# Perceiver block kernel: query transposes and two maxima products of the second cross attention placed ahead of the first scores

## The chip, the cores and the metric

One core of one Trainium2 chip runs the whole kernel as one program. The metric is the device time of one execution in microseconds; the time before is the median of three runs. TensorE is called PE, VectorE DVE, ScalarE ACT and GpSimd POOL; SP issues most DMAs.

## The reference, cut to what matters

The model has two layers, each with a cross attention, a self attention and a mixture of experts. The change lies in the second layer's cross attention, with 512 tokens (8 batches of 64), a context of 1601 rows a batch, 16 heads of width 16, and one key and value head that all query heads share:

```
q = x @ Wq
kv = context @ Wkv
k, v = jnp.split(kv, 2, axis=-1)
q = q.reshape(b, n, h, hd).transpose(0, 2, 1, 3) * scale
sim = jnp.einsum('bhnd,btd->bhnt', q, k)
att = jax.nn.softmax(sim, axis=-1)
y = jnp.einsum('bhnt,btd->bhnd', att, v)
return y.transpose(0, 2, 1, 3).reshape(b, n, d) @ Wo
```

## The kernel before, in words

Every engine has its own list of instructions, written out by hand in order; semaphores (`mq[...]` in this stage) tie them together. There is no planner: the order in the source is the order of each engine.

Queries are split in parts of bfloat16 (`Qs`, 96 columns a head), turned by PE with the heads' columns on partitions, and copied by ACT from PSUM into `QT`. Token tile t (0 to 3) has 16 heads, turned in two halves, `turn_queries(t, h8, at)`: 8 transposes of 128 by 96 into bank `at`; ACT's `queries_turned` copies them (L750). Tile 0 is turned first, since everything needs it. The other six turns are in `QUERY_TURNS`, one at the end of each of the units 0 to 5, all into bank 6; so each waits for the copy of the one before.

A group g (0 to 15, `NH`) is 8 heads of one batch. The softmax's maximum for each group is found by `maxima`: 13 chunks (`CH`) of products of queries and keys, 12 of four matmuls with 512 columns (L1670) and a short one of 16 with 65 columns (L1676), alternately in banks 4 and 5. DVE reduces each (L1096, the short one L1098), and chunk n waits until the reduce of chunk n - 2 is done. After the 13th reduce DVE takes the negative maximum (L1106); for group 0 DVE splits it in two bfloat16 parts (L1109, L1110), for the others POOL does (L516, L517). `rows(g)` turns the parts into two more rows by PE (L1690, bank 6), ACT copies them behind the queries (`row`, L767), so that `scores` gives the scores less their maximum.

A unit u is a seventh (`HS`) of a group: `scores(u)` has 8 matmuls of 512 columns (L1702) in banks 0, 1 or 2, 3, ACT takes the exponential (L789), `values(u)` multiplies by the values (L1716). Loop pass u issues scores(u + 1), one maxima chunk, values(u - 1), the other chunks, and then the turn. `chunks_by(u)` says how many chunks are issued by the end of pass u: 13 before the loop, then 16, 19, 22, 25, 28, 31, 33 and on. At s_ = 5 of each group `rows(g + 1)` goes ahead of the scores.

Before the loop PE projects the queries, turns tile 0, and alternates the projections of the tiles 1 to 3 with two chunks each; then it runs chunks 8 to 12, `keep_clock(7, 7)` (7 matmuls of 128x512 into bank 7 that nobody reads, L1282), `rows(0)`, `keep_clock(2, 7)` and `scores(0)`. POOL prepares the parts of the tiles 1 to 3 meanwhile (L503 to L511).

Of the kernel before, what the change touches and what calls it, by code (L numbers as in the profile page):

```python
# [16 lines left out]
TT = TOK // P  # L17
# [12 lines left out]
NH, HS = 2 * NB, 7  # L30
# [3 lines left out]
CH = 13  # L34
# [24 lines left out]
def build(nc, a, out, scratch_x, scratch_y, scratch_g):  # L59
    with ExitStack() as ctx:  # L60
# [136 lines left out]
        def bank(i, n=512):  # L197
            return ps[:, i, 0:n]
# [12 lines left out]

        def chunks_by(u):

            return min(CH * NH, CH + 3 * (u + 1), 20 + -(-CH * (u + 1) // HS))

        QUERY_TURNS = {(0, s_): (1 + s_ // 2, s_ % 2) for s_ in range(2 * TT - 2)}

        def key_tiles(s):
            return [k for k in (2 * s, 2 * s + 1) if k < KT_N]
# [2 lines left out]
        def sems(prefix, names):  # L222
            return {n: sem(f"{prefix}_{n}") for n in names.split()}
# [21 lines left out]
        at = sems("attn", "sc z ex pt_ps pt pv y v0")  # L245
# [28 lines left out]
        mq = sems("mq", "neg ln xt_ps xt q_ps qhi qf qs qdup qt_ps qt qt_b a_ps a_max nm row_ps row s_ps exp pv o o_ps y y_ps yt out_ps x")  # L274
# [280 lines left out]
        def _(act):  # L555
# [181 lines left out]
            def scaled_queries(t):  # L737
                act.wait_ge(mq["q_ps"], t + 1)
                q_ps = bank((7, 6, 7, 0)[t], D).rearrange("p (h d) -> p h d", h=H)
                if t == 0:  # L740
                    act.mul(Qs[:, 0:H, 0:HD], q_ps, SCALE).then_inc(mq["qhi"], 1)
                    act.wait_ge(mq["qhi"], 1)
                    act.activation(Qs[:, 0:H, HD:2 * HD], Qs[:, 0:H, 0:HD], ACT.Copy).then_inc(mq["qf"], 1)
                    return
                act.mul(qf[:, t * H:(t + 1) * H, :], q_ps, SCALE)
                act.mul(Qs[:, t * H:(t + 1) * H, 0:HD], q_ps, SCALE).then_inc(mq["qf"], 1)

            def queries_turned(t, h8, at):
                act.wait_ge(mq["qt_ps"], 2 * t + h8 + 1)
                act.activation(QT[0:KQ, 2 * t:2 * t + 2, 8 * h8:8 * h8 + 8, :].rearrange("p b h q -> p h b q"),  # L750
                               ps[0:KQ, at, :].bitcast(BF16).rearrange("p (h b q) -> p h b q", h=8, b=2), ACT.Copy).then_inc(mq["qt"], 1)
# [9 lines left out]
            for t in range(1, TT):  # L761
                scaled_queries(t)
            act.activation(exp_warm[:], xnT[:, 0, 0:1], ACT.Exp)

            def row(g):
                act.wait_ge(mq["row_ps"], g + 1)
                act.activation(QT[KQ:KQ2, g // 2, 8 * (g % 2):8 * (g % 2) + 8, :],  # L767
                               ps[KQ:KQ2, 6, :].rearrange("p (h q) -> p h q", h=8), ACT.Copy).then_inc(mq["row"], 1)

            def sums_out(g):  # L770
                act.wait_ge(mq["pv"], HS * (g + 1))
                if g >= 2:
                    act.wait_ge(mq["o_ps"], g - 1)
                act.activation(oT[g % 2], bank(7, P), ACT.Copy).then_inc(mq["o"], 1)
# [6 lines left out]
            for g in range(NH):  # L781
                for s_ in range(HS):
                    u = g * HS + s_
# [7 lines left out]
                    if s_ == 0 and g >= 1:  # L791
                        sums_out(g - 1)
                    if (g, s_ - 1) in QUERY_TURNS:
                        queries_turned(*QUERY_TURNS[g, s_ - 1], 6)
                    if s_ == 4 and g >= 2 and g % 2 == 0:
# [49 lines left out]
        def _(dve):  # L845
# [277 lines left out]
            def add_out(t):  # L1123
                dve.wait_ge(mq["out_ps"], t + 1)
                dve.tensor_tensor(x[:, t, :], bank(4 + t % 2, D), x[:, t, :], ALU.add).then_inc(mq["x"], 1)

            maxima(0, chunks_by(-1))
            for u in range(NH * HS):
                maxima(chunks_by(u - 1), chunks_by(u))
                if u >= HS and u % HS == 2:  # L1130
                    outputs(u // HS - 1)
# [147 lines left out]
        def _(pe):  # L1279
            def keep_clock(n, at):  # L1280
                for _ in range(n):
                    pe.matmul(bank(at), ident_b, mask_b, start=True, stop=True, skip_group_check=True)  # L1282
# [360 lines left out]
            def turn_queries(t, h8, at):  # L1643
                if t == 0:
                    pe.wait_ge(mq["qs"], 2)
                    pe.wait_ge(mq["qf"], 1)
                else:
                    pe.wait_ge(mq["qt"], 2 * t + h8)
                pe.wait_ge(mq["qdup"], t + 1)
                for i in range(8):  # L1650
                    to, j = (6, i - 4) if (t, h8) == (0, 0) and i >= 4 else (at, i)
                    ins = pe.transpose(ps[0:KQ, to, :].bitcast(BF16)[:, j * P:(j + 1) * P], Qs[:, t * H + 8 * h8 + i, :], ident_b)
                ins.then_inc(mq["qt_ps"], 1)

            def maxima(lo_, hi_):

                for n in range(lo_, hi_):
                    g, j = n // CH, n % CH
                    b, r = g // 2, g % 2
                    if j == 0:  # L1660
                        pe.wait_ge(mq["qt"], 2 * (b // 2) + r + 1)
                    if n == 6:
                        pe.wait_ge(mq["qt_b"], 1)
                    if n >= 2:
                        pe.wait_ge(mq["a_max"], n - 1)
                    at = 4 + n % 2
                    if j < CH - 1:
                        h, c = 8 * r + 2 * (j // 3), j % 3
                        for i in range(4):
                            ins = pe.matmul(ps[32 * i:32 * i + 32, at, :], QT[0:KQ, b, h + i // 2, 32 * (i % 2):32 * (i % 2) + 32],  # L1670
                                            kT[0:KQ, b, 512 * c:512 * c + 512], start=True, stop=True, skip_group_check=True)
                    else:
                        for q in range(4):
                            for i in range(4):
                                h = 8 * r + 2 * q + i // 2
                                ins = pe.matmul(ps[32 * i:32 * i + 32, at, q * REM_AT:q * REM_AT + REM],  # L1676
                                                QT[0:KQ, b, h, 32 * (i % 2):32 * (i % 2) + 32],
                                                kT[0:KQ, b, REM0:S], start=True, stop=True, skip_group_check=True)
                    ins.then_inc(mq["a_ps"], 1)

            def rows(g):
                pe.wait_ge(mq["nm"], g + 1)
                if g >= 1:
                    pe.wait_ge(mq["row"], g)
                if g >= 2:
                    pe.wait_ge(mq["y"], g - 1)
                if g >= 3:
                    pe.wait_ge(mq["yt"], (g - 1) // 2)
                for q in range(4):
                    ins = pe.matmul(ps[KQ:KQ2, 6, q * P:(q + 1) * P], NM[g % 2][:, q, :], ident_b, start=True, stop=True, skip_group_check=True)  # L1690
                ins.then_inc(mq["row_ps"], 1)
# [29 lines left out]
            def turn_out(g):  # L1721
                pe.wait_ge(mq["o"], g + 1)
                pe.wait_ge(mq["row"], min(g + 2, NH))
                pe.wait_ge(mq["qt"], min(2 * TT, 2 + sum(at <= (g + 1, 1) for at in QUERY_TURNS)))
                pe.transpose(ps[:, 6, 0:P], oT[g % 2], ident).then_inc(mq["o_ps"], 1)

            def turn_y(b):
# [11 lines left out]
            for c in range(C):  # L1739
                for t in range(1, TT):  # L1740
                    ins = pe.transpose(ps[:, c, (t - 1) * P:t * P], xn[:, t, c * P:(c + 1) * P], ident)
                ins.then_inc(mq["xt_ps"], 1)
            turn_queries(0, 0, 2)
            turn_queries(0, 1, 3)
            maxima(0, 2)
            for t in range(1, TT):
                queries(t)
                maxima(2 * t, 2 * t + 2)
            maxima(2 * TT, chunks_by(-1))
            pe.wait_ge(mq["qf"], TT)  # L1750
            keep_clock(7, 7)
            rows(0)
            keep_clock(2, 7)
            scores(0)
            for u in range(NH * HS):
                g, s_ = u // HS, u % HS
# [10 lines left out]
                maxima(min(hi_, lo_ + 1), hi_)  # L1767
                if (g, s_) in QUERY_TURNS:
                    turn_queries(*QUERY_TURNS[g, s_], 6)
                if s_ == 1 and g >= 1:  # L1770
                    turn_out(g - 1)
                if g == NH - 1 and 1 <= s_ <= TT - 1:
                    project_out(s_ - 1)
            values(NH * HS - 1)
            turn_out(NH - 1)
            turn_y(NB - 1)
            project_out(TT - 1)
# [88 lines left out]
            def turn_block(j):  # L1866
                for i, (lo_, _) in enumerate(XG):
                    if j == lo_:
                        pe.wait_ge(xg_in[i], 16)
                if j >= 1:  # L1870
                    pe.wait_ge(m1["xgt"], j)
                for c in range(C):
                    ins = pe.transpose(ps[:, 0, c * P:(c + 1) * P], xg[:, j, c * P:(c + 1) * P], ident)
                ins.then_inc(m1["xg_ps"], 1)
# [113 lines left out]
```

## Time and profile before

| | us |
|---|---|
| median of 3 runs | 569.2 |
| lowest, highest | 567.25, 570.67 |
| the profiled execution, its time | 570.37 |
| its span | 568.2 |
| PE busy | 524.9 (92%) |
| DVE busy | 325.6 (57%) |
| ACT busy | 300.4 (53%) |
| POOL busy | 124.1 (22%) |

A matmul's busy time overlaps that of the next, and so a busy PE is not PE at its peak. The second cross attention lies between 237 and 415 us of the span.

### The profile page before, as it was taken

Reading aid. Unit: us, or ns where it says so; the run is one execution under the profiler, and the core shown is the slowest. Engines: PE = TensorE matmul, PEld = TensorE weight load, DVE = VectorE, ACT = ScalarE, POOL = GpSimd, SP = SyncE. Lnnn points to the kernel's source line nnn. Section 1 sums busy time; section 2 is a strip of 40 time slices with the busy share of each in tenths; the row PEclk is TensorE's granted clock in tenths of the full one; section 3 lists DMA queues with packets and bytes.
Section 4 is the critical chain, followed back from the end, with each engine's and each line's share of the span. In section 5 each row is a group of like instructions: output and inputs, shape, how many; then the busy total and the mean of one; then the engine's idle time right before and its main releaser. Section 6 shows DMA issues by size and latency. Waiting matters only on the chain.

```text
span 568.2 us, 15207 instructions
## 1 busy us (share of the span) xinstructions
PE 524.9 (92%) x6433; PEld 367.2 (65%) x6433; DVE 325.6 (57%) x671; ACT 300.4 (53%) x511; POOL 124.1 (22%) x217
## 2 busy tenths in 40 slices
PE   3899999769999999789999999999979979999994
PEld 2657667435666666435676767676556647999993
DVE  4454573434666666567998989898146684011101
ACT  0346556635656666257887878777714412333330
POOL 5104404613333344250000000000060043000004
PEclk9899999969999999999999999999989998999999
DMA  8916603503555554550000000000080001998812
GB/s 312 396 40 221 234 12 91 180 14 107 153 155 151 146 160 132 175 196 3 2 3 4 3 3 3 2 4 4 2 298 1 2 1 38 240 380 275 292 38 92
DMA packets 35362, 64.89 MB, mean 114 GB/s; under 512 B 3328, under 2 KB 24832, under 8 KB 34912
## 3 DMA queue, kind: packets, MB, share of 16 engines
q1 hardware_dynamic: 34768, 62.87, 33.7%
q8 instruction: 51, 0.84, 0.6%
q0 software_dynamic: 384, 1.05, 0.6%
q14 instruction: 15, 0.12, 0.1%
q10 hardware_dynamic: 144, 0.01, 0.0%
HBM read 59.92 MB, written 4.00 MB: 112 GB/s over the span
## 4 chain that ended last, share of the span: by engine, by line
PE 82%; DVE 7%; DMA 4%; POOL 3%; ACT 2%; issue 2%; SPq 0%; POOLq 0%; DVEq 0%; ACTq 0%
PE ps L1316 15%; PE ps L1593 10%; PE ps L1702 9%; PE ps L1670 8%; PE ps L1615 7%; PE ps L1716 7%; PE ps L1894 6%; PE ps L1417 4%; PE ps L1294 2%; PE ps L1430 2%; PE ps L1443 2%; PE ps L1397 2%; DVE region L1096 2%; DMA ctx64T<-in_ctx64T 1%; PE ps L1282 1%
## 5 line engine op out<-in xcount | busy, mean ns | idle before, releaser
L1096 DVE TENSOR_REDUCE region<-ps 128x1 f32<-128x512 f32 x192 | 124.1, 688 | 18.0 <-PE ps L1670 18.0
L789 ACT ACTIVATE region<-ps 128x1024 f32<-128x1024 f32 (+1 forms) x112 | 105.9, 963 | 19.7 <-PE ps L1702 19.2
L1670 PE MATMUL ps<-ctx_kT,region 96*32 96x512 bf16 x768 | 82.1, 383 | 2.6 <-DVE region L1096 1.8
L1702 PE MATMUL ps<-region,ctx_kT 98*32 98x512 bf16 x832 | 72.5, 381 | 0.6 <-ACT region L767 0.4
L1716 PE MATMUL ps<-region,ctx_v 128*32 128x128 f32 (+1 forms) x1664 | 70.2, 272 | 0.0
L1593 PE MATMUL ps<-region 128*128 128x512 f16 x264 | 65.1, 392 | 1.3 <-ACT ctx_kT L576 0.8
L1716 PEld LDWEIGHTS ps<-region,ctx_v 128*32 128x32 f32 (+1 forms) x1664 | 56.7, 109 | 9.5 <-issue 0.3
L839 ACT ACTIVATE region<-ps,ctx_v 128x128 f32<-128x128 f32 x88 | 25.2, 368 | 57.1 <-PE ps L1316 57.1
L494 POOL TENSOR_TENSOR region<-region 128x512 f32<-128x512 f32 x33 | 38.1, 1156 | 76.1 <-ACT region L732 74.7
L1615 PE MATMUL ps<-region 128*128 128x256 bf16 x396 | 48.7, 273 | 2.4 <-DVE region L1048 2.4
L1615 PEld LDWEIGHTS ps<-region 128*128 128x128 bf16 x396 | 38.5, 98 | 14.3 <-DVE region L1048 3.5
L1593 PEld LDWEIGHTS ps<-region 128*128 128x128 bf16 x264 | 26.2, 101 | 28.7 <-issue 4.2
L1056 DVE SCALAR_TENSOR_TENSOR region<-ps,region 128x512 f32<-128x512 f32 x33 | 22.8, 691 | 33.3 <-PE ps L1593 30.9
L1670 PEld LDWEIGHTS ps<-ctx_kT,region 96*32 96x32 bf16 x768 | 23.4, 94 | 28.0 <-DVE region L1096 17.1
L1316 PEld LDWEIGHTS ps<-region 128*128 128x128 f32 x288 | 33.3, 192 | 0.3
L1316 PE MATMUL ps<-region 128*128 128x128 f32 x288 | 33.4, 274 | 0.0
L516 POOL CAST region<-region 128x4 bf16<-128x4 f32 x15 | 2.9, 190 | 137.8 <-DVE region L1106 137.8
L717 ACT ACTIVATE region<-region 128x512 bf16<-128x512 f32 x33 | 20.8, 631 | 21.2 <-POOL region L494 21.2
L732 ACT ACTIVATE region<-region 128x512 bf16<-128x512 f32 x33 | 20.8, 630 | 19.3 <-DVE region L1066 19.2
L1702 PEld LDWEIGHTS ps<-region,ctx_kT 98*32 98x32 bf16 x832 | 24.9, 96 | 7.7 <-ACT region L767 1.3
L1268 DVE TENSOR_TENSOR region<-ps,ctx_v 128x256 f32<-128x256 f32 x11 | 4.7, 425 | 36.9 <-PE ps L1894 36.9
L904 DVE TENSOR_REDUCE region<-ps 128x8 f32<-128x512 f32 x24 | 16.5, 688 | 16.1 <-PE ps L1417 16.1
(224 smaller groups left out, 842.2 us busy)
## 6 DMA issues: line engine op xcount, KB each, us to landing
region<-in_w SPq DMA_DIRECT2D x15, 1024.0 KB, 8.7
region<-in_ctxT SPq DMA_DIRECT2D x8, 1601.0 KB, 7.7
region<-gates SPq DMA_DIRECT2D x32, 256.0 KB, 3.5
ctx_kT<-in_w SPq DMA_DIRECT2D x7, 1024.0 KB, 7.5
region<-in_moe SPq DMA_DIRECT2D x33, 192.0 KB, 2.4
attn_weights<-in_wall SPq DMA_DIRECT2D x1, 2152.0 KB, 22.8
slots_x<-zeros SPq DMA_DIRECT2D x1, 1408.0 KB, 10.5
ctx_v<-in_b2row SPq DMA_DIRECT2D x1, 1024.0 KB, 5.0
```

The source lines that it names most:

```text
L494: pool.tensor_tensor(hr[n % 2], t2[n % 2], hp[n % 4][0], ALU.subtract).then_inc(m0["r"], 1)
L789: act.activation(probs[u % NP_][:, 0:512 * n_keys], ps[:, pr:pr + n_keys, :].rearrange("p b n -> p (b n)"), ACT.Exp).then_inc(mq["exp"], 1)
L839: ins = act.activation(hT[j % 2][:, k, :], ps[:, (1, 6)[j % 2] + hh, (k % 4) * P:(k % 4 + 1) * P], ACT.Gelu, bias=b1_s[:, j, k:k + 1])
L1056: ins = dve.scalar_tensor_tensor(out=dst, in0=bank(2 + n % 2), scalar=1.0 / XS, in1=sa[n % 2], op0=ALU.mult, op1=ALU.mult)
L1096: ins = dve.tensor_reduce(mp[g % 2][:, j // 3, j % 3:j % 3 + 1], bank(4 + n % 2), AX.X, ALU.max)
L1316: ins = pe.matmul(dst, lhs(c), rhs(c), start=(c == 0), stop=(c == C - 1))
L1593: ins = pe.matmul(bank(dst), wn[:, c * 256 + half * 128:c * 256 + half * 128 + 128], xp[k][:, c, :], start=(c == 0 and k == 0), stop=(c == ...
L1615: ins = pe.matmul(ps[:, 6 + t // 2, (t % 2) * D:(t % 2) * D + D], hp[n % 4][k][:, t * P:(t + 1) * P], w0[n % 4][:, 512:768], start=(n == 0 ...
L1670: ins = pe.matmul(ps[32 * i:32 * i + 32, at, :], QT[0:KQ, b, h + i // 2, 32 * (i % 2):32 * (i % 2) + 32], kT[0:KQ, b, 512 * c:512 * c + 51 ...
L1702: ins = pe.matmul(ps[32 * c:32 * c + 32, 2 * (u % 2) + i, :], kT[0:KQ2, b, k * P + 32 * c:k * P + 32 * c + 32], QT[0:KQ2, b, 8 * r:8 * r + ...
L1716: ins = pe.matmul(ps[32 * c:32 * c + 32, 7, 0:P], v_ctx[0:rows_, b, k, :], probs[u % NP_][0:rows_, 512 * i + P * c:512 * i + P * (c + 1)], ...
L1894: ins = pe.matmul(bank(3 + j % 2, D), hT[j % 2][:, k, :], w2_s[j % WSLOTS][:, k, :], start=(k == 0), stop=(k == HC - 1))
```

## The change

Three of the six later turns, (1, 0), (1, 1) and (2, 0), go ahead of the loop, behind the chunks 9, 10 and 12, into the banks 2, 3 and 1; ACT copies them right after the projections' copies. The chunks 13 and 14 go ahead of the loop as well, so that `chunks_by(-1)` is 15 and `chunks_by(0)` stays 16. The three turns left are in the units 0, 1 and 2; the units 3, 4 and 5 have none. The 7 unread matmuls ahead of `rows(0)` are taken out; the 2 behind it stay.

```
-            return min(CH * NH, CH + 3 * (u + 1), 20 + -(-CH * (u + 1) // HS))
-        QUERY_TURNS = {(0, s_): (1 + s_ // 2, s_ % 2) for s_ in range(2 * TT - 2)}
+            return min(CH * NH, CH + max(2, 3 * (u + 1)), 20 + -(-CH * (u + 1) // HS))
+        EARLY_TURNS = {10: (1, 0, 2), 11: (1, 1, 3), 13: (2, 0, 1)}
+        QUERY_TURNS = {(0, 0): (2, 1), (0, 1): (3, 0), (0, 2): (3, 1)}
...
             act.activation(exp_warm[:], xnT[:, 0, 0:1], ACT.Exp)
+            for turn in EARLY_TURNS.values():
+                queries_turned(*turn)
...
-                    pe.wait_ge(mq["qt"], 2 * t + h8)
+                    pe.wait_ge(mq["qt"], 2 * t + h8 if at == 6 else 2)
...
-                pe.wait_ge(mq["qt"], min(2 * TT, 2 + sum(at <= (g + 1, 1) for at in QUERY_TURNS)))
+                pe.wait_ge(mq["qt"], min(2 * TT, 2 + len(EARLY_TURNS) + sum(at <= (g + 1, 1) for at in QUERY_TURNS)))
...
-            maxima(2 * TT, chunks_by(-1))
+            for n in range(2 * TT, chunks_by(-1)):
+                maxima(n, n + 1)
+                if n + 1 in EARLY_TURNS:
+                    turn_queries(*EARLY_TURNS[n + 1])
             pe.wait_ge(mq["qf"], TT)
-            keep_clock(7, 7)
             rows(0)
             keep_clock(2, 7)
             scores(0)
```

## Rows read from the trace of the kernel before

**Rows 1.** The page, part 4: shares of the chain that ended last.

```profile
PE 82%; DVE 7%; DMA 4%; POOL 3%; ACT 2%; issue 2%; SPq 0%; POOLq 0%; DVEq 0%; ACTq 0%
```

**Rows 2.** The chain of waits, 235 to 415 us: start us, us, what.

```profile
250.85 1.62 PE ps L1282 x7
```

**Rows 3.** Timeline ahead of the scores: start us, us, engine, line, operation [idle before].

```profile
247.40 3.69 DVE L1096 TENSOR_REDUCE region<-ps 128x1 f32<-128x512 f32 x6 [0.32 <-PE ps L1670]
...
248.74 0.40 PE L1670 MATMUL ps<-ctx_kT,region 96*32 96x512 bf16 x4 [0.20 <-DVE region L1096]
...
250.54 0.31 PE L1676 MATMUL ps<-ctx_kT,region 96*32 96x65 bf16 x16 [0.20 <-DVE region L1096]
...
251.00 0.42 DVE L1098 TENSOR_REDUCE region<-ps 128x4 f32<-128x260 f32 x1
...
251.87 0.17 DVE L1110 TENSOR_TENSOR region<-region 128x4 bf16<-128x4 f32 x1
...
252.40 0.38 PE L1690 MATMUL ps<-const_bf,region 128*2 128x128 bf16 x4
...
252.82 0.59 ACT L767 ACTIVATE region<-ps 2x512 bf16<-2x512 f32 x1 [3.59 <-PE ps L1690]
...
253.46 1.05 PE L1702 MATMUL ps<-region,ctx_kT 98*32 98x512 bf16 x16
...
254.12 1.94 ACT L789 ACTIVATE region<-ps 128x1024 f32<-128x1024 f32 x2 [0.72 <-PE ps L1702]
...
254.77 1.89 DVE L1096 TENSOR_REDUCE region<-ps 128x1 f32<-128x512 f32 x3 [2.74 <-PE ps L1670]
```

**Rows 4.** The chain of waits, 256 to 270 us, one unit of it.

```profile
256.50 0.55 PE ps L1702 x8
257.04 0.25 PE ps L1670 x4
...
257.31 0.70 DVE region L1096
...
258.06 0.40 PE ps L1670 x4
258.46 0.58 PE ps L1652 x8
```

**Rows 5.** Timeline of units with a turn.

```profile
256.43 0.61 PE L1702 MATMUL ps<-region,ctx_kT 98*32 98x512 bf16 x8
...
258.39 0.65 PE L1652 MATMUL ps<-const_bf,region 128*96 128x128 bf16 x8
...
258.97 0.62 PE L1702 MATMUL ps<-region,ctx_kT 98*32 98x512 bf16 x8
259.07 1.02 ACT L750 ACTIVATE region<-ps 96x1024 bf16<-96x1024 bf16 x1 [0.61 <-PE ps L1652]
...
259.85 1.94 DVE L1096 TENSOR_REDUCE region<-ps 128x1 f32<-128x512 f32 x3 [0.59 <-PE ps L1670]
```

**Rows 6.** Timeline from unit 4 to unit 6.

```profile
264.87 0.43 DVE L1098 TENSOR_REDUCE region<-ps 128x4 f32<-128x260 f32 x1 [0.53 <-PE ps L1676]
...
265.84 0.20 POOL L517 TENSOR_TENSOR region<-region 128x4 bf16<-128x4 f32 x1
...
266.26 0.22 PE L1690 MATMUL ps<-const_bf,region 128*2 128x128 bf16 x1
...
268.78 0.61 PE L1702 MATMUL ps<-region,ctx_kT 98*32 98x512 bf16 x8
...
269.66 3.86 DVE L1096 TENSOR_REDUCE region<-ps 128x1 f32<-128x512 f32 x6 [0.59 <-PE ps L1670]
```

**Rows 7.** Stretches: us, busy (count) of PE, PEld, DVE, ACT, POOL, granted clock, DMA.

```profile
248.00:254.00 6.00, 4.92 (x57) 1.84 (x61) 3.93 (x10) 1.81 (x3) 4.96 (x12) 1.00 0.14 53
256.00:270.00 14.00, 13.45 (x272) 8.39 (x275) 10.66 (x19) 11.12 (x14) 0.40 (x2) 1.00 0.02 4
115.00:130.00 15.00, 11.36 (x53) 5.35 (x54) 4.78 (x16) 5.34 (x8) 2.05 (x4) 0.66 0.02 5
```

## The prediction

> **What bounds the kernel now.** I read the page first: TensorE (PE) is busy 92% of the span and has 82% of the chain that ended last [rows 1]. That is an average, and the change touches only some 20 us out of 568, so the next view was the chain inside this stretch, and then the instructions in order of time on both sides of the first scores.
>
> Ahead of the scores, PE and VectorE (DVE) hand the maxima products to and fro in banks 4 and 5. Chunks 8 to 11 start every 0.60 us and the reduces run at the same pace: six in 3.69 us, so (3.69 - 0.69) / 5 = 0.60 each [rows 3]. The reader is to see that there is no slack here: chunk 9 starts at 248.74 and takes about 0.45 us to be readable (as the short one from 250.54 to 251.00), 249.19, and its reduce, the fourth from 247.40 on, starts at 249.20. Chunks 8, 10 and 11 follow the same pattern. Then chunk 12 and its reduce at 251.00, the small operations to 252.04 (the maxima's negative in two parts), `rows(0)` at 252.40, ScalarE's (ACT) copy at 252.82, scores(0) at 253.46 [rows 3]. Two things stand out. The chain of waits goes through the 7 unread products, not through DVE's small operations [rows 2]: `rows(0)` could have begun at about 252.10. And DVE is idle for 2.74 us before the reduce at 254.77 [rows 3].
>
> After the scores have begun, each unit with a query turn costs 2.54 us (scores start at 256.43, the next at 258.97) [rows 5]. The chain of one unit is: turn 0.58, scores 0.55, first maxima chunk 0.25, its reduce 0.70, third chunk 0.40, and the turn again [rows 4]; four such units repeat it. The third chunk needs the first one's bank, and the turn and the scores stand behind it, so DVE's three reduces (1.95 us) and PE's own turn can't overlap fully: DVE idles 0.59 us in each such unit [rows 5].
>
> **The change, part by part.** Units are numbered by the loop's u, and all times are in the profiled execution (570.37 us, span 568.2, so 2.2 us around it).
>
> *Two turns inside the maxima run (after chunks 9 and 10).* A turn begins 0.33 us after the chunk before it starts (258.06 to 258.39) and the next product begins 0.58 us later [rows 5], so a chunk behind a turn starts 0.91 us after the one before. Chunk 10: 248.74 + 0.91 = 249.65 in place of 249.34. Its reduce: 250.10 in place of 249.80. Chunk 11, behind the second turn: 249.65 + 0.91 = 250.56, readable at 251.01, in place of 250.40: +0.61. Chunk 12 waits for reduce 10, 250.85, and its reduce for reduce 11, 251.61 in place of 251.00. So the small operations end at 252.65. The turns' own waits are for the copies of tile 0, done before the first chunk, and for POOL's parts of their tile, which the timeline shows ready earlier than each turn; behind a waiting turn the next chunk would stand, and DVE for it.
>
> *The third turn, and chunks 13 and 14.* The turn follows chunk 12: 251.2 to 251.8. Chunk 13 at about 251.8, chunk 14 when reduce 12 has freed bank 4, at 252.1. All of it lies beside DVE's tail, which ends at 252.65, and on DVE the two reduces come behind the small operations, in the 2.74 us hole. Cost on the path: nothing. If that cover went, chunk 14 would hold `rows(0)` by at most one chunk, 0.2 us.
>
> *The 7 unread products go.* `rows(0)` begins right behind DVE: 252.65 + 0.06 = 252.71 against 252.40. So of +0.61 from the turns 0.30 comes back: together **+0.31**. Bounds of this stage: 0 (if the turns fill PE's gaps without moving a reduce) and +0.9 (two turns at 0.81 us with their weight wait, less 0.3, and some for the third).
>
> *ACT's three copies of 1.02 us before row(0).* Back to back, operations of this size follow each other in 0.92 us (two in 1.94 [rows 3]). A copy starts 0.68 us after its turn [rows 5]: 249.75, 250.68, and the third 251.88 to 252.81. The row copy is due at 252.71 + 0.42 = 253.13, so ACT is free 0.3 us before it is needed. Cost: nothing; if the third turn came 0.5 us late, 0.2 us.
>
> Scores(0) starts at 253.77 in place of 253.46.
>
> *Unit 0 with one chunk in place of three.* Before, scores(2) start 2.97 us after scores(0) (253.46 to 256.43), since the third chunk waits for a reduce. Now: 16 scores matmuls in four rounds of four, (1.05 - 0.40) / 3 = 0.22 each, put chunk 15 at +0.87; the turn comes 0.33 later, scores(2) 0.58 later: 1.78, at 255.55, just behind the end of the first exponential (254.43 + 1.02). **-1.19**; difference so far -0.88.
>
> *Units 1 and 2* still have a turn and three chunks: 2.54 us each, as before. Scores(4) at 260.65 in place of 261.51. ACT has two pieces of 0.93 in each and isn't late.
>
> *Units 3, 4 and 5 without a turn.* What is late next is DVE: three reduces at 0.63 us, 1.9 us a unit. Unit 3: its first reduce at 261.54, unit 4's first at 263.43, after 1.89, where before it was 2.48 (the first reduce of unit 4 at 264.87 [rows 6], that of unit 3 at 259.85 + 2.54 [rows 5]): **-0.6**. Unit 4 holds the short chunk 25, whose four row maxima must reach `rows(1)` by way of POOL before scores(6). Before, POOL's second part was ready 1.17 us after that chunk's reduce began (264.87 to 266.04), and `rows(1)` came at 266.26, behind the turn, 1.39 after it [rows 6]. Now `rows(1)` can begin at 263.43 + 1.17 + 0.06 = 264.66, with PE standing idle for half a us: a wait takes the turn's place, and only 1.39 - 1.23, **-0.16**, is left. Unit 5: the reduce of chunk 28 to that of chunk 31 in 1.89 us, against the 2.54 of a unit with a turn: **-0.65**. Scores(7) then start at about 266.5 against 268.77 [rows 6].
>
> Sum: +0.31 - 1.19 - 0.60 - 0.16 - 0.65 = **-2.29**.
>
> *Afterwards* chunk numbers per unit are the same as before, and DVE's lag behind PE as well: scores(7) stood 0.89 us before the reduce of chunk 31, now 0.92. So the rest of the stage moves by the same amount. No DMA or queue entry is moved past another; the expert weights come relative to PE's progress.
>
> One rule of the Trainium skill speaks against the change. First the trace: with one turn of 8 transposes in each 2.54 us, 256 to 270, the granted clock was 1.00, and it was 1.00 in 248 to 254, where PE had its sparse maxima and the 9 unread products [rows 7]. The Trainium skill, "TensorE: Matmul & The Clock Gate", Part 4: PE-mode transpose, says that a transpose doesn't count as busy PE in the way a matmul does, and does not by itself bring the full clock. By it, the turns are no replacement for unread matmuls, and the clock may fall just as the scores start, which gives the time of rival A; by the rows, where one maxima chunk per 0.60 us already held it, my sum stands.
>
> **Rivals.**
>
> *A. The clock falls (slower).* Place: from about 252 on, because real matmul columns are gone from 250.8 to 252.4. Price: the longest stretch at 1.2 GHz in this trace lasts 10.2 us (115 to 130 at a mean of 0.66: 0.34 / 0.5 x 15) [rows 7]. In a unit with a turn PE is taken for about 2.0 us out of 2.54 (all but its wait for the reduce, by the chain [rows 4]); at half the clock for 4.0, so each unit takes some 1.5 us more, in 4.0 us of time. A stretch of 10.2 us costs 3.8: -2.3 + 3.8 = +1.5, that is 570.7 us in terms of the median. It turns slower at a stretch of about 6 us. For it: what stands in place of the products is mostly transposes. Against it: PE's columns from 248 to 254 are as many as before (three turns and two chunks, about 1.7 us, against 7 products, 1.6), and maxima alone didn't lose it. Chance 0.07.
>
> *B. The gain stays in the first units only.* The later units' gain is given back, because DVE is bound with rows(1) or at unit 7, or because the turns cost +0.9 in front. Of the sum -0.88 is left where the units 3 to 5 give theirs back, and -1.67 where the front costs 0.6 more; by the first, 568.3. For it: DVE runs six reduces without a gap from 269.66 [rows 6]. Against it: the lag worked out above. Chance 0.2.
>
> *C. DVE alone sets the pace.* From the first reduce after the row copy to that of chunk 31, DVE's work is 15 long reduces and the short one, 15 x 0.63 and some 0.65, 10.1 us; starting at 255.1 (chunk 15 of unit 0 and 0.45) it would reach 265.2 in place of 269.66: -4.4, 564.8. For it: the exponentials no longer share ACT with the turns from unit 3 on. Against it: units 1 and 2 keep the full 2.54. Something between this and my sum, -3 to -4.4, has 0.15.
>
> *D. Nothing moves*, because another wait (weights, ACT) holds the stage: 569.2. Against it: the chain runs through just these instructions [rows 2, 4]. Chance 0.08.
>
> My forecast has the remaining 0.5.
>
> **How the numbers follow.** The forecast is 570.37 - 2.3 = 568.1 for the profiled execution. That one lay 1.2 above the median of 569.2, and the three runs spread over 3.4 us (567.25 to 570.67), so I give 569.2 - 2.2 = **567.0**. That is 0.4%. A measurement of this kernel tells about 0.5% (2.85 us) from no change; so my own likeliest case sits on the "same" side of that line, and C, with the deeper part of mine, on the "faster" side: with a spread of about 1.5 us on the difference of medians, a third of my case and nearly all of C: 0.36 faster. Slower by over 0.5% needs A at its longest or an unlucky pair of medians: 0.07. The rest, 0.57, is same. Range: C's lower end, 564.6, to D with some of A, 570.0.
>
> **What would show it.** Scores(0) about 0.3 us later; no PE wait on unread products before `rows(0)`; two reduces within the 2.74 us hole; scores(0) to scores(2) 1.8 us; two units of 2.54 and then three near 1.9; `rows(1)` with an idle PE of half a us ahead; scores(7) 2.3 us earlier at an equal start; granted clock 1.00 in 248 to 270. What would make it wrong: a clock under 1.00 there, a row copy waiting for ACT, or a steady part of a different length than before.

## The result, and the profile after

| | before | changed |
|---|---|---|
| median, us | 569.41 (6 runs, 567.25 to 571.07) | 565.26 (6 runs, 564.01 to 567.07) |
| ratio | | 0.9936, 95% interval 0.9909 to 0.9964 |
| profiled execution, span | 568.2 | 561.9 |
| PE, DVE, ACT busy | 524.9, 325.6, 300.4 | 520.9, 325.7, 300.1 |

A second set of 12 runs of the changed kernel, in a later job (e8 below), gave 565.92 us and a ratio of 0.9948 (0.9929 to 0.9967). By the two ratios the change gains 3.0 to 3.6 us (0.5 to 0.6%); the two medians of the table lie 4.15 us apart, and I go by the ratios, which the intervals belong to. I had forecast 2.2, and 567.0.

The two spans differ by 6.3 us, and most of that isn't the change. Chunk 6's reduce, ahead of anything that was edited, already starts 1.68 us earlier (247.40 and 245.72). So I measure the stretch from that reduce to scores(7), within each profile. It is 21.38 us before and 19.35 after: **-2.03**. From scores(10) to the last scores both kernels need 136.5 us, and nothing is given back. The 2.6 us that are left lie behind the attention, in code that didn't change; e8 below shows what they are.

The timeline of the changed kernel ahead of the scores (line numbers are 3 higher than before; ACT's L750 is L751), which answers to [rows 3]:

```profile
245.72 2.49 DVE L1099 TENSOR_REDUCE region<-ps 128x1 f32<-128x512 f32 x4 [0.32 <-PE ps L1673]
...
247.07 0.40 PE L1673 MATMUL ps<-ctx_kT,region 96*32 96x512 bf16 x4 [0.20 <-DVE region L1099]
...
247.40 0.65 PE L1655 MATMUL ps<-const_bf,region 128*96 128x128 bf16 x8
...
247.97 0.40 PE L1673 MATMUL ps<-ctx_kT,region 96*32 96x512 bf16 x4
248.08 3.03 ACT L751 ACTIVATE region<-ps 96x1024 bf16<-96x1024 bf16 x3 [0.53 <-PE ps L1655]
...
248.88 0.40 PE L1673 MATMUL ps<-ctx_kT,region 96*32 96x512 bf16 x4
...
249.94 0.42 DVE L1101 TENSOR_REDUCE region<-ps 128x4 f32<-128x260 f32 x1
...
250.60 0.30 DVE L1112 CAST region<-region 128x4 bf16<-128x4 f32 x1
...
250.93 0.30 DVE L1113 TENSOR_TENSOR region<-region 128x4 bf16<-128x4 f32 x1
251.14 1.27 DVE L1099 TENSOR_REDUCE region<-ps 128x1 f32<-128x512 f32 x2
...
251.37 0.38 PE L1693 MATMUL ps<-const_bf,region 128*2 128x128 bf16 x4 [0.56 <-DVE region L1113]
...
251.79 0.59 ACT L770 ACTIVATE region<-ps 2x512 bf16<-2x512 f32 x1 [0.68 <-PE ps L1693]
...
252.43 1.05 PE L1705 MATMUL ps<-region,ctx_kT 98*32 98x512 bf16 x16
```

A chunk behind a turn starts 0.90 us after the one before it (247.07, 247.97, 248.88), as worked out. The reduce of chunk 12 is 4.22 after chunk 6's, against 3.60 before [rows 3]: +0.62. The two reduces of 251.14 fill DVE's hole. ACT has the row copy ready in time. What I had not foreseen: the two small operations take 0.30 us each and not 0.17.

Chain of waits of the changed kernel, from the last unit with a turn to unit 5 (start us, us, what), which answers to [rows 4]:

```profile
258.38 0.40 PE ps L1673 x4
258.78 0.58 PE ps L1655 x8
259.35 0.55 PE ps L1705 x8
259.90 0.25 PE ps L1673 x4
260.15 0.02 issue
260.17 1.95 DVE region L1099 x3
262.12 0.35 DVE region L1101
...
262.49 0.18 DVE region L1109
...
262.99 0.21 POOL region L518
...
263.25 0.22 PE ps L1693
```

The turn is gone from the chain, DVE's reduces take its place, and for `rows(1)` the chain passes through POOL, with PE waiting. Step by step, in us after chunk 6's reduce:

| | before | changed | step | forecast |
|---|---|---|---|---|
| scores(0) | 6.06 | 6.71 | +0.65 | +0.31 |
| scores(2) | 9.03 | 8.48 | -1.20 | -1.19 |
| scores(4) | 14.11 | 13.56 | 0.00 | 0 |
| scores(5) | 16.65 | 15.42 | -0.68 | -0.60 |
| scores(6) | 18.88 | 17.54 | -0.11 | -0.16 |
| scores(7) | 21.38 | 19.35 | -0.69 | -0.65 |
| sum | | | -2.03 | -2.29 |

The clock of the changed kernel in the stretch and just behind it (us, busy (count) of PE, PEld, DVE, ACT, POOL, granted clock, DMA), beside [rows 7]:

```profile
248.00:254.00 6.00, 5.19 (x81) 2.74 (x81) 4.13 (x10) 4.44 (x5) 3.40 (x8) 1.00 0.02 5
254.00:262.00 8.00, 7.57 (x165) 4.33 (x167) 6.16 (x10) 6.91 (x9) 0.00 (x0) 1.00 0.01 2
```

So the stretch gave 2.0 us, and the runs 3.0 to 3.6. The experiments had to settle two things: whether the parts add as in the table, and where the other 1.0 to 1.6 us are.

### The profile page after: what moved, and what is told of

Its sections match the earlier page's. It is cut to its first block, busy times and chain, and to the rows that moved or that the text cites. A ratio compares the mean times of both kernels' runs of the same rounds, so it can differ in the third digit from the quotient of the medians.

```text
span 561.9 us, 15194 instructions
## 1 busy us (share of the span) xinstructions
PE 520.9 (93%) x6426; PEld 364.2 (65%) x6426; DVE 325.7 (58%) x671; ACT 300.1 (53%) x511; POOL 123.9 (22%) x217
## 4 chain that ended last, share of the span: by engine, by line
PE 82%; DVE 7%; POOL 3%; ACT 3%; DMA 2%; issue 2%; another core or an unknown queue 1%; SPq 0%; POOLq 0%; DVEq 0%; ACTq 0%
PE ps L1319 15%; PE ps L1596 10%; PE ps L1705 9%; PE ps L1673 8%; PE ps L1618 7%; PE ps L1719 7%; PE ps L1899 6%; PE ps L1420 4%; PE ps L1433 2%; PE ps L1446 2%; PE ps L1297 2%; PE ps L1400 2%; DVE region L1099 1%; DMA ctx64T<-in_ctx64T 1%; PE ps L1314 1%
## 5 line engine op out<-in xcount | busy, mean ns | idle before, releaser
L1059 DVE SCALAR_TENSOR_TENSOR region<-ps,region 128x512 f32<-128x512 f32 x33 | 22.8, 691 | 32.7 <-PE ps L1596 30.4
```

The costliest lines, as they stand in the source:

```text
L1059: ins = dve.scalar_tensor_tensor(out=dst, in0=bank(2 + n % 2), scalar=1.0 / XS, in1=sa[n % 2], op0=ALU.mult, op1=ALU.mult)
```

## The experiments

In all of them "the stretch" is chunk 6's reduce to scores(7). e1 to e4 ran together, then e5, e6, e8 and e9, then e7, e10, e11 and e12, each time with the kernel before beside them on the same chip. The three groups ran on three different chips, so a median is compared with that of the kernel before in its own group.

**e1: the turns without the chunks.**

```
 changed kernel, chunks_by:
-    CH + max(2, 3 * (u + 1))
+    CH + 3 * (u + 1)
```

> The three early turns as in the changed kernel and the 7 unread products gone, but the chunks 13 and 14 back in unit 0. Theory (the steps of the prediction, with the trace of after): front +0.65 us against the kernel before, unit 0 no gain (scores(2) about 3.0 us after scores(0)), units 3 to 5 still -1.5: the stretch from chunk 6's reduce to scores(7) is 0.8 us shorter than before and 1.2 longer than in the changed kernel; median 568.6. Rival (the two chunks are hidden anyway, the turns bring it all): 2.0 us shorter, as the changed kernel.

The stretch was 20.55 us (-0.83 against before), scores(0) to scores(2) 2.97, units 3 to 5 as in the changed kernel. Median 567.97, ratio 0.9979 (0.9960 to 0.9999). The theory holds; the two chunks are worth 1.2 us.

**e2: the chunks without the turns, without unread products.**

```
 kernel before:
-    CH + 3 * (u + 1)
+    CH + max(2, 3 * (u + 1))
...
-            keep_clock(7, 7)
```

> The chunks 13 and 14 ahead of the loop and the 7 unread products gone, but all six turns in the units 0 to 5. Theory: front -0.3 us against before, unit 0 -1.2, units 1 to 5 at 2.54 us as before: the stretch is 1.5 us shorter, median 567.9. Rival (all the gain comes with the turns): under 0.5 us shorter. Rival (clock): with neither turns nor unread products in front the granted clock falls below 1.00 between 248 and 262.

A miss for the theory and a hit for its clock rival. The stretch took 22.11, 0.73 longer than before, and the granted clock was 0.50 from 248.0 on for 6.8 us:

```profile
248.00:254.00 6.00, 5.72 (x57) 2.18 (x58) 3.09 (x8) 2.43 (x3) 2.50 (x6) 0.50 0.01 3
```

Median 568.09, ratio 0.9992 (0.9968 to 1.0017). The lower clock began 3.2 us after chunk 6's reduce, which is before the place where the 7 products had stood, so their absence can't have brought it; e9 tests that.

**e3: the kernel before without the 7 unread products.**

```
-            keep_clock(7, 7)
```

> The kernel before without the 7 unread products alone. Theory: the stretch is 0.3 us shorter (rows(0) starts 0.06 us behind DVE's small operations), clock 1.00, median 569.1. Rival (clock): a stretch at 1.2 GHz starts between 250 and 256 and costs 1.3 us or more.

`rows(0)` came 0.22 us earlier, but 3.4 us at the lower clock began at 250.5; the stretch took 22.53, 1.15 longer than before:

```profile
248.00:254.00 6.00, 4.29 (x50) 1.48 (x50) 2.16 (x7) 1.62 (x3) 3.34 (x8) 0.72 0.01 2
```

Median 569.66, ratio 1.0015 (0.9994 to 1.0035). A miss for the theory, and a hit for its rival. Here the lower clock began 4.9 us after chunk 6's reduce; in the kernel before the products run from 3.4 to 5.1 us after it. And the 12 runs had more time at the lower clock than the kernel before (30.7 us against 24.9, table below). So taking out the products alone gains nothing, and they seem to be worth something for the clock from their own place on.

**e4: the products put back into the changed kernel.**

```
             pe.wait_ge(mq["qf"], TT)
+            keep_clock(7, 7)
             rows(0)
```

> The changed kernel with the 7 unread products put back ahead of rows(0). Theory: rows(0) starts 0.8 us later than in the changed kernel (7 x 0.22 behind chunk 14, less PE's idle time there), the rest of the stage unchanged: 1.2 us shorter than before in the stretch, median 568.2 by the stretch alone. If the rest of the measured gain (-3.6 measured, -2.0 in the stretch) comes with the changed kernel's early start of the later stages, a part of it goes here too; if it is a draw of slow-clock stretches per execution, the profile's stretches at 1.2 GHz lie elsewhere without order.

`rows(0)` came 0.99 us later than in the changed kernel, all steps behind it were the same, the stretch was 20.34 (-1.04 against before) and the clock 1.00. Median 567.17, ratio 0.9958 (0.9938 to 0.9977). So with the turns in front the products only cost. Here too the runs gained more (2.4 us) than the stretch (1.0).

**e8: the changed kernel again.**

> The changed kernel once more, for more runs and a second profile. If the stretch accounts for all of the gain, the ratio against before is near 0.9964 (-2.0 us). If the later stages truly run faster when they start 3.7 us earlier, near 0.9936 again, and the profile again has no stretch at 1.2 GHz near 465. If that absence was a draw, such a stretch of 6.8 us may be there again.

The stretch was 19.38 us, as in the changed kernel's first profile to 0.03. A piece at 1.2 GHz near 465 was there this time (462.5, 6.8 us), so its absence in the first profile was a draw. From the last scores to the warming of the Gelu table (L828 before) the kernel before took 60.97, 59.50 and 61.08 us in its three profiles, the changed one 59.11 and 59.18.

All fourteen profiles show what the 2.6 us behind the attention are. Two pieces at 1.2 GHz come and go there, one of 3.4 us that begins between 409 and 421, and one of 6.8 us that begins between 462 and 469. From the last scores to the end of the span it is 158.2 to 159.0 us in the eight profiles that have both (all three of the kernel before, e1, e2, e4, e5, e6), 157.3 to 157.4 in the four without the first (e3, e7, e8, e9), and 155.9 and 156.1 in the two without the second (e10 and the changed kernel's first), whatever the kernel. So the 2.6 us are the luck of one profile and no gain of the change.

The ratio, 0.9948, still lies below the 0.9964 of the stretch alone, though its interval (0.9929 to 0.9967) just holds it.

**e9: the chunks, with the products kept.**

```
 kernel before:
-    CH + 3 * (u + 1)
+    CH + max(2, 3 * (u + 1))
```

> The kernel before with the chunks 13 and 14 ahead of the loop, the 7 unread products kept behind them, and all six turns in the units. Theory (the chunks are worth 1.19 us in unit 0 as long as the clock stays): clock 1.00 in this stretch, rows(0) 0.5 us later than before (two chunks' columns, 0.44), scores(0) to scores(2) 1.8 us, scores(7) about 0.7 us earlier than before, 20.7 after chunk 6's reduce. Rival (the loss of the run without unread products had another cause than the clock): no gain here either, 21.4 or more.

A miss: the clock fell all the same, at 249.3 for 6.8 us, 3.0 us after chunk 6's reduce and so before the 7 products. `rows(0)` came 2.9 us later than in the kernel before, behind these products at half speed, scores(0) to scores(2) took 1.98 us, and the stretch 23.72. That is more than the rival's 21.4, but by the clock, which the rival had excluded. Median 568.59, ratio 0.9991 (0.9965 to 1.0017): in most runs all this can't have cost that much. This run gave the idea that 7 products after the maxima run don't protect the run itself, and that the kernel before may lose the clock there too, in some executions.

**e10: filled maxima run.** One unread product is put behind each of the chunks 8 to 11 of the kernel before.

```
-            maxima(2 * TT, chunks_by(-1))
+            for n in range(2 * TT, chunks_by(-1)):
+                maxima(n, n + 1)
+                if n < CH - 1:
+                    keep_clock(1, 1)
```

> The kernel before with one unread product more behind each of the chunks 8 to 11, the 7 kept, nothing moved. Theory (the part of the gain that no profile of the stretch shows is slow clock that the sparse maxima run brings in a share of the executions, and PE work inside the run prevents it): mean time at the lower clock per execution 22 to 23 us as in the kernels with early turns, against 24.8 before; scores(7) 21.4 to 22.0 after chunk 6's reduce; the time 0 to 1 us lower than before. Rival (the later stages run faster because they start earlier): time at the lower clock as before, 24.8, the time higher by what the fillers cost.

The stretch was 21.61 us (0.23 longer), and yet the median 567.62 against 569.75, ratio 0.9965 (0.9943 to 0.9988): four products more, and the kernel was 2.0 us faster. The theory had 0 to 1 us for this. The time at the lower clock is in the table below. The profile shows no piece at 1.2 GHz in the stretch, but neither do two of the three of the kernel before; so no run shows where in the execution the 2.0 us come from. The stretch is longer because DVE's last small operation took 0.56 us in place of 0.17, beside POOL, and `rows(0)` waited for it:

```profile
249.28 0.67 POOL L506 TENSOR_TENSOR region<-region 128x256 bf16<-128x256 f32 x1
249.41 0.56 DVE L1110 TENSOR_TENSOR region<-region 128x4 bf16<-128x4 f32 x1
```

**e11 and e12: the kernel before, two more profiles.**

> The kernel before once more, for its profile. By the theory of e10 a stretch at 1.2 GHz lies between 245 and 262 us in some of its executions, and scores(7) then come 22.5 us or more after chunk 6's reduce. By the rival the stretch is 21.38 long in each of its profiles, at clock 1.00.

> The same as e11: a third profile of the kernel before. A stretch at 1.2 GHz between 245 and 262 us, and scores(7) at 22.5 us or more, in one of e11 and e12 at least if it comes in half of the executions; in neither if the clock holds there always.

e11: stretch 21.38, clock 1.00. e12: stretch 22.95. PE in e12, to be read beside the 7 products of 1.62 us in [rows 2]:

```profile
249.51 0.40 PE L1670 MATMUL ps<-ctx_kT,region 96*32 96x512 bf16 x4 [0.20 <-DVE region L1096]
250.11 0.41 PE L1676 MATMUL ps<-ctx_kT,region 96*32 96x65 bf16 x16 [0.20 <-DVE region L1096]
250.45 3.16 PE L1282 MATMUL ps<-const_bf 128*128 128x512 bf16 x7
253.54 0.38 PE L1690 MATMUL ps<-const_bf,region 128*2 128x128 bf16 x4
```

and its clock:

```profile
248.00:254.00 6.00, 5.20 (x44) 1.75 (x41) 3.51 (x9) 0.82 (x3) 4.61 (x11) 0.72 0.06 20
```

The clock was lost at 250.1, just as chunk 12 began and 3.1 us after chunk 6's reduce. The 7 products, issued from 250.45 on and all at half speed, held `rows(0)` for 1.57 us more. So the kernel before does have this loss, in one of its three profiles.

Each run of the three groups lists its span and mean granted clock; 2 x (1 - clock) x span is its time at 1.2 GHz:

| kernels | runs | mean us at 1.2 GHz (standard error) | profiles with such a piece at 245 to 262 |
|---|---|---|---|
| before | 89 | 24.9 (0.3) | 1 of 3 |
| e3, no products | 12 | 30.7 (1.2) | 1 of 1 |
| e2, chunks only | 12 | 27.3 (0.9) | 1 of 1 |
| e9, chunks, products | 12 | 25.8 (0.7) | 1 of 1 |
| changed, both sets | 18 | 22.8 (0.5) | 0 of 2 |
| the five others with early turns | 54 | 23.0 (0.5) | 0 of 5 |
| e10, filled run | 12 | 21.9 (1.2) | 0 of 1 |

The changed kernel has 2.1 us less at the lower clock per execution. In e12 3.4 us of it, in the stretch, cost 1.57; at that price the 2.1 us are 1.0 us of time, and with the 2.0 of the stretch that makes 3.0. This is an estimate, and not shown. The table counts the lower clock wherever it lies in the execution, 1 of 3 profiles against 0 of 7 can be chance, and within the kernel before a run with more time at the lower clock was hardly slower: the 27 runs with about 22.7 us of it took 569.8 us in the mean, the 36 with about 26.1 took 569.5, and over all 87 the time rises by 0.10 us for each us (standard error 0.07).

Nor is the excess of the runs over the stretch special to the changed kernel. By their ratios all eleven sets, e10 and those without early turns too, did better than their stretch says against 21.38, by 0.3 (e3) to 2.9 us (e9). The mean stretch of the three profiles of the kernel before is 21.90, which takes 0.5 us of each; the rest has no measured cause.

**e6: POOL held back.** For the 0.30 us operations.

```
                 pool.wait_ge(mq["qf" if t else "qhi"], t + 1)
+                if t == TT - 1:
+                    pool.wait_ge(mq["nm"], 1)
```

> The changed kernel with POOL's preparation of tile 3 held back until group 0's maxima are through, so that POOL is idle beside DVE's small operations. If POOL is what makes the two small ones take 0.30 in place of 0.17 us: they take 0.17 and scores(0) comes 0.26 us earlier (6.45 after chunk 6's reduce against 6.71). If ACT's copies are the cause: 0.30 still, scores(0) at 6.71. In both cases tile 3 is ready by unit 0's turn.

DVE in e6 (start us, us, line, operation):

```profile
249.99 0.17 DVE L1114 CAST region<-region 128x4 bf16<-128x4 f32 x1
250.19 0.17 DVE L1115 TENSOR_TENSOR region<-region 128x4 bf16<-128x4 f32 x1
```

They took 0.17 us each, scores(0) came at 6.45, and the stretch was 19.10, just as expected of POOL as the cause, while ACT copied as before. In the changed kernel POOL ran these beside the two operations at 250.60 and 250.93:

```profile
250.19 0.67 POOL L507 TENSOR_TENSOR region<-region 128x256 bf16<-128x256 f32 x1
...
250.81 0.39 POOL L508 COPY region<-region 128x256 bf16<-128x256 bf16 x1
```

Median 566.16, ratio 0.9939 (0.9915 to 0.9962): 0.25 us can't be seen in the runs.

**e5: four early turns.**

```
-        EARLY_TURNS = {10: (1, 0, 2), 11: (1, 1, 3), 13: (2, 0, 1)}
-        QUERY_TURNS = {(0, 0): (2, 1), (0, 1): (3, 0), (0, 2): (3, 1)}
+        EARLY_TURNS = {9: (1, 0, 2), 10: (1, 1, 3), 12: (2, 0, 1), 13: (2, 1, 0)}
+        QUERY_TURNS = {(0, 0): (3, 0), (0, 1): (3, 1)}
...
                     pe.wait_ge(mq["qt"], 2 * t + h8 if at == 6 else 2)
+                    if at == 0:
+                        pe.wait_ge(mq["qf"], TT)
```

> Four turns ahead of the scores (behind the chunks 8, 9, 11 and 12), only two left, in the units 0 and 1. Theory (a turn inside the maxima run costs 0.3 us, one behind chunk 12 nothing, and each one taken out of a unit gives 0.6): scores(0) 0.3 us later than in the changed kernel, unit 2 at 1.9 in place of 2.5 us, scores(7) 19.05 us after chunk 6's reduce against 19.35 in the changed kernel and 21.38 before. Rival (ACT's four copies or POOL's parts of tile 2 hold the front): scores(0) 0.9 us or more later, no gain.

Better than expected: scores(0) at 6.73, no later than in the changed kernel, unit 2 at 1.85, stretch 18.70 (-2.68 against before). The timeline shows why the third turn cost nothing. Chunk 11 now follows chunk 10 directly, its bank being free, and DVE reduces the two without a gap, the second 0.60 behind the first; so chunk 12, behind the turn, is there just when DVE is (its reduce 4.22 after chunk 6's, as in the changed kernel):

```profile
249.06 0.69 PE L1675 MATMUL ps<-ctx_kT,region 96*32 96x512 bf16 x8
249.51 1.29 DVE L1099 TENSOR_REDUCE region<-ps 128x1 f32<-128x512 f32 x2 [0.21 <-PE ps L1675]
```

Median 565.08, ratio 0.9929 (0.9906 to 0.9951), the lowest of all, though the 0.65 us to the changed kernel lie within the noise of the runs; the profiles alone show them.

**e7: e5 and e6 together.**

> Four turns ahead of the scores and POOL's tile 3 held back, together. The two gains lie on different pieces (unit 2, and DVE's small operations) and should add: scores(7) 18.70 - 0.27 = 18.43 us after chunk 6's reduce (changed kernel 19.35, before 21.38), 0.9 us faster than the changed kernel, ratio against before about 0.993. Rival (tile 3 is now late for the turn in unit 0): PE waits in unit 0 and scores(2) comes over 1.8 us after scores(0).

A miss: stretch 19.19, not 18.43. The rival came true. With four turns in front, the turn in unit 0 is one of tile 3, and POOL, started late, holds it:

```profile
255.07 0.62 PE L1659 MATMUL ps<-const_bf,region 128*96 128x128 bf16 x8 [0.73 <-POOL region L514]
```

Unit 0 took 2.54 us again. Median 566.69, ratio 0.9947 (0.9924 to 0.9971).

## Why the prediction was right, and where it was not

The range held, and the direction. Of the steps:

- *Two turns inside the maxima run:* right in place and size (+0.62 at chunk 12's reduce for +0.61). Their waits were met. But e5 moves three turns into this run for no more than two cost, so "0.3 each" isn't a general price: a turn costs what it makes DVE wait, and the third made it wait for nothing.
- *The 7 unread products go:* the release was right (`rows(0)` now waits for DVE alone), the size not: +0.65 in place of +0.31. 0.26 of the difference is DVE's two small operations beside POOL, shown by e6, and about 0.08 a later start of `rows(0)`. The trace of before had shown them at 0.17 with POOL busy as well, so I saw no reason to doubt it. What differs is which instruction was first: in the trace of before POOL's subtraction (L506) begins 0.01 us behind DVE's last small operation; in the changed kernel POOL is already at work when DVE's two begin, and each ends 0.02 to 0.03 us after POOL's. So the front, +0.31, is the term of the sum that was mis-sized most.
- *ACT's three copies:* at no cost, as said; they began at 248.08 and the row copy wasn't held.
- *Unit 0, units 3 to 5, the wait for POOL at `rows(1)`:* right within 0.08 each; e1 shows the chunks' part by itself.
- *Afterwards:* right; 136.5 us from scores(10) to the last scores in both.
- *The clock* is the step in which the reasoning was wrong, though the number held. I read 1.00 in [rows 7] as "the maxima run already held the clock", and gave the clock only to the changed kernel, as a loss (rival A). It was one execution. In this stretch the lower clock was seen in one of three profiles of the kernel before (e12), in e2, e3 and e9, and in none of seven with turns there. If this adds to the gain, by about 1.0 us as estimated above, it is most of what my forecast fell short by (0.8 to 1.4 us); the runs don't show that it does. The rule of the Trainium skill that I weighed ("TensorE: Matmul & The Clock Gate", Part 4: PE-mode transpose), that a transpose doesn't by itself bring the full clock, did not decide here: in six of those seven profiles the transposes stood in for unread matmuls, between maxima matmuls, at clock 1.00 (e4 has both), and no run here has transposes alone.

Rivals B and D are excluded by the steps. C (DVE alone) came true in units 3 and 5 only, where it was part of my sum. So 2.0 us of the gain are shown step by step, and 1.0 to 1.6 us stay open. They may lie outside the stretch altogether. Chunk 6's reduce, ahead of every edit, starts at 246.5 to 247.4 us in the three profiles of the kernel before and at 244.8 to 246.6 in the eleven others; but the three executions profiled were 0.9 us slower in the mean than the kernel's median, so this can be luck too. What share of the executions of the kernel before loses the clock in the stretch stays open, as does why a single execution is hit.

## What to carry to other kernels

Moving work from a unit where it sits on the chain into a wait of another engine gained nearly the full period here, 1.2 us for two chunks and 0.6 us a turn, until the next engine was full. In e9 and e12 the clock fell inside the sparse stretch, before the unread matmuls behind it had begun, so such matmuls can't guard it from there; whether they do inside it, e10 suggests but doesn't show, and real work that is due anyway stood in for them in six profiles. Where a clock is in play one profile is one draw: compare several profiles, and the time at the lower clock over many runs, before saying that a stretch holds it, and then look whether that time is felt in the runs at all.

## What the runs showed of the hardware that I had not expected

- DVE's two small operations (128x4) lasted until POOL's instruction that was already running had ended, and 0.02 to 0.03 us more: 0.30 us each in the changed kernel, 0.56 for the second in e10 and 0.67 in e9, where POOL's subtraction (L506) had begun 0.13 and 0.02 us earlier. They took 0.17 where POOL was idle (e6), and where POOL's subtraction began just after the second (before). The reduce in front of them (L1106, in the changed kernel L1109) took 0.17 with that subtraction under way too.
- The kernel with four more matmuls ran faster (e10, 0.9965). Its runs had 21.9 us at the lower clock against 24.9, but that this is the cause isn't shown.
- Unread matmuls issued after the sparse run did not keep the clock: it fell 0.3 us before the first of them, and the 7 then took 3.16 us in place of 1.62 (e12).
